# Decoder layer on one core: routing's norm and turns of 12 of 16 token tiles moved into the cross-attention stage

## The chip, the cores and the metric

One core of a Trainium2 chip. The metric is the device time of one execution in microseconds; lower is better. TensorE (PE), VectorE (DVE), ScalarE (ACT), GpSimd (POOL) and SyncE (SP) run their own instruction lists and meet in semaphores; 16 DMA engines move the data.

## The reference

```python
x = x + attention(_layernorm(x), ...)        # 16 heads, ternary weights, int8-like activations
x = x + cross_attention(_layernorm(x), ctx_1024, Wq, Wk, Wv, Wo, gq, gk)   # 16 heads of 128
xf = _layernorm(x).reshape(-1, 256)
logits = xf @ router_w.T                     # 8 experts
top_v, top_i = jax.lax.top_k(logits, 2)
combine = sum(one_hot(top_i, 8) * softmax(top_v)[..., None], axis=1)
y = einsum('etf,ehf->eth', silu(xf @ gate_w[e].T) * (xf @ up_w[e].T), down_w)
x = x + einsum('te,eth->th', combine, y)
```

x is 32 x 64 x 256 in float32: 2048 tokens, 16 tiles (`NT`) of 128 tokens by 256 channels. F is 688. Float32 accuracy is kept by writing a number as a sum of two float16 halves and taking three of the four products.

## The kernel before

Three stages follow each other, each an `nc.Block` in which every engine has its own list, and a barrier between them.

`attention` (to about 209 us) is not touched.

`cross_attention` works on 4 groups (`NG`) of 4 tiles. Two heads of a group make a pair, 8 pairs (`NU`) a group, 32 pairs in all. A loop over steps N from -9 to 32 is written out for each engine by hand, and the order of the calls in it is the order on the engine. In step N the pair N+9 is projected (queries, keys), pair N+1 gets its scores and softmax, and pair N is multiplied with the context and projected out (`project_out`). For N from 24 (`TAIL`) no projections are left: these are the tail's steps, in which the turned probabilities come from TensorE and ScalarE (`turn_p`, `turned_copy`) and not from a DMA. After the last pair of a group VectorE adds the result to x (`residual`, steps 8, 16, 24, 32), and SyncE saves the group's rows of x to the output (`save_group`).

Beside it the weights of the experts are split in 67 pieces of 128x512: SyncE loads a piece, ScalarE makes the high half (`piece_high`), VectorE or GpSimd the low half (`piece_low`; odd ones, and the first 16 both, on GpSimd), SyncE saves both halves to `w_hl` and then issues the load of a later piece (`piece_save`, L795). Two pieces belong to each step from -8 (`piece_at`, L709), so the last, 66, falls into step 25. On ScalarE `piece_high` stands at the head of a step (L1045 to L1050). On SyncE the norms of the keys go out and come back broadcast (`key_norms_out`, `key_norms_in`) behind the step's saves; GpSimd's `both_norms` waits for them, and its `quotient` stands behind that. In step 26 SyncE loads the down weights of four experts (`first_down_weights`).

`experts` begins with routing. VectorE takes the moments of all 16 tiles (`token_stats`), ScalarE the root, VectorE writes the normed rows to `ao` (L1649). TensorE turns them in pairs of tiles in float32 (L1778), ScalarE copies the turned tiles out, TensorE multiplies with the router's weights (L1786); between these stand products whose result nobody reads (`idle_work`, L1765). ScalarE and VectorE split the rows in halves (L1595, L1653), and two DMAs save them to `h_rows` (L1599). A chain on VectorE picks the top two and gives each token a place in one of 39 slots of 128 rows. SyncE has issued the gate and up weights at the stage's start (L1520); ScalarE issues the down weights of the other four experts once the top two are known (L1603 to L1607). Then for every slot: GpSimd gathers the rows (L1557), SyncE turns them (L1525), TensorE multiplies with gate and up (L1825) and down (L1841), and GpSimd adds the result to the output (L1572).

## Time and profile before

| | us |
|---|---|
| median of 3 runs | 852.17 (851.31 to 855.72) |
| profiled execution | 852.5 |
| its span | 850.4 |
| step -1 of cross-attention | 260.61 to 274.44 |
| tail, from the first turn to the last product | 517.99 to 569.3 |
| routing, from the moments to the first expert product | 570.89 to 622.79 |

Times in the rows count from the span's start. Busy shares over the span are PE 85%, DVE 67%, ACT 53%, POOL 45%; they mix stages with different limits.

### The profile page before, as it was taken

The numbers are of one execution on the slowest core, as the hardware profiler recorded it, in microseconds if no ns is written. First come the engines' busy times: TensorE is split into PE (matmuls) and PEld (weight loads), VectorE is DVE, ScalarE is ACT, GpSimd is POOL, SyncE is SP. The second block draws the span as 40 slices with busy tenths as digits, with TensorE's granted clock in tenths as the row PEclk, the third lists the DMA queues.
The fourth block names the chain that finished last, engine by engine and source line by source line (L and its number), as shares of the span: only waits on it lengthen the run. The fifth ranks groups of instructions, "written<-read, shape, count | busy, mean of one in ns | idle before, by whom it ended". The sixth has DMA issues, their size and how long they took to land. (4 is left out here: it accounts for less than half of the span.)

```text
span 850.4 us, 26921 instructions
## 1 busy us (share of the span) xinstructions
PE 722.7 (85%) x10796; PEld 522.1 (61%) x10796; DVE 568.7 (67%) x1052; ACT 453.9 (53%) x875; POOL 382.5 (45%) x462
## 2 busy tenths in 40 slices
PE   0499888887887999999999996988199999998993
PEld 0388777775443566656556664766167777776772
DVE  5778788863886989999898997967853333332330
ACT  0567777764785666667675763544023333333331
POOL 0112222322585555555555555620056666665753
PEclk9879999995998999999999998999599999999997
DMA  9312222321664757576757573619949988889882
GB/s 323 112 50 56 59 52 64 66 58 20 168 194 156 186 127 180 135 187 160 191 128 173 163 167 112 223 31 406 369 89 158 149 147 143 142 128 137 145 140 40
DMA packets 192471, 121.91 MB, mean 143 GB/s; under 512 B 140800, under 2 KB 172800, under 8 KB 192224
## 3 DMA queue, kind: packets, MB, share of 16 engines
q1 hardware_dynamic: 178928, 103.54, 50.3%
q0 software_dynamic: 7488, 9.32, 7.1%
q10 hardware_dynamic: 5936, 7.34, 2.5%
q8 instruction: 90, 1.47, 0.7%
q14 instruction: 29, 0.24, 0.1%
HBM read 61.04 MB, written 27.00 MB: 104 GB/s over the span
## 5 line engine op out<-in xcount | busy, mean ns | idle before, releaser
L1754 DVE SCALAR_TENSOR_TENSOR f_slot_work<-psu,f_slot_work 128x688 f32<-128x688 f32 x39 | 34.1, 875 | 109.8 <-PE psu L1825 109.8
L1350 PE MATMUL xbank_a<-arena,x_o 128*128 128x256 f16 x768 | 96.6, 277 | 5.7 <-DVE x_o L1155 2.9
L1572 POOL DMA_INDIRECT out_dram<-f_y,f_to x39 | 62.2, 1595 | 71.8 <-DMA out_dram<-f_y,f_to 55.4
L1350 PEld LDWEIGHTS xbank_a<-arena,x_o 128*128 128x128 f16 x768 | 73.4, 99 | 28.7 <-DVE x_o L1155 10.3
L1254 PE MATMUL xbank_qk<-arena 128*128 128x512 f16 x336 | 84.8, 390 | 4.6 <-PEq L188 4.3
L1841 PE MATMUL fbank<-arena,f_slot_work 128*128 x663 | 79.2, 274 | 3.3 <-DMA f_slot_work<-hid_hl 3.3
L1825 PE MATMUL psg<-wgu,f_slot_work 128*128 x468 | 74.7, 309 | 2.5 <-DMA f_slot_work<-rows_in 2.0
L1825 PE MATMUL psu<-wgu,f_slot_work 128*128 x468 | 74.6, 309 | 0.0
L1841 PEld LDWEIGHTS fbank<-arena,f_slot_work 128*128 128x128 f16 x663 | 64.7, 98 | 14.6 <-issue 4.3
L1622 ACT CAST hid_hl<-f_slot_work 128x688 f16<-128x688 f32 x39 | 29.8, 765 | 77.4 <-DVE f_slot_work L1754 75.4
L915 POOL TENSOR_TENSOR arena<-arena,cst 128x512 f32<-128x512 f32 x25 | 26.0, 1039 | 92.2 <-DVE cT L1190 92.2
L961 ACT ACTIVATE sqq<-xbank_qk 128x512 f32<-128x512 f32 x56 | 33.3, 595 | 56.3 <-PE xbank_qk L1254 56.3
L1615 ACT ACTIVATE f_slot_work<-psg 128x688 f32<-128x688 f32 x39 | 29.0, 743 | 64.4 <-PE psg L1825 63.1
L545 PE MATMUL bank_pt<-cst,sp 64*64 64x64 f32 x1024 | 42.8, 242 | 21.6 <-ACT pT L321 19.4
L1825 PEld LDWEIGHTS psg<-wgu,f_slot_work 128*128 128x128 f16 x468 | 45.4, 98 | 23.4 <-issue 3.8
L1825 PEld LDWEIGHTS psu<-wgu,f_slot_work 128*128 128x128 f16 x468 | 45.8, 98 | 22.5
L1757 DVE TENSOR_TENSOR hid_hl<-f_slot_work,hid_hl 128x688 f16<-128x688 f32 x39 | 34.2, 877 | 32.4 <-ACT hid_hl L1622 32.4
L545 PEld LDWEIGHTS bank_pt<-cst,sp 64*64 64x64 f32 x1024 | 38.4, 154 | 23.9 <-issue 20.5
L1254 PEld LDWEIGHTS xbank_qk<-arena 128*128 128x128 f16 x336 | 28.7, 99 | 36.8 <-issue 8.0
L1145 DVE TENSOR_TENSOR q_hl<-xbank_qk,q_hl 128x512 f16<-128x512 f32 x56 | 38.4, 686 | 16.9 <-ACT q_hl L962 16.9
L1262 PE MATMUL xbank_qk<-cT,wk 128*128 128x512 f16 x168 | 47.1, 391 | 0.0
L904 POOL TENSOR_TENSOR x_pf<-x_sc,x_rden 128x512 f32<-128x512 f32 x32 | 33.4, 1042 | 29.8 <-DVE x_rden L1178 29.8
(285 smaller groups left out, 1717.5 us busy)
## 6 DMA issues: line engine op xcount, KB each, us to landing
arena<-in_wx SPq DMA_DIRECT2D x51, 256.0 KB, 3.0
wgu<-w_hl SPq DMA_DIRECT2D x2, 5504.0 KB, 26.5
ao<-key_norms SPq DMA_DIRECT2D x64, 128.0 KB, 3.3
w_hl<-cT SPq DMA_DIRECT2D x26, 256.0 KB, 2.1
w_hl<-x_pair SPq DMA_DIRECT2D x25, 256.0 KB, 2.2
ao<-in_wx SPq DMA_DIRECT2D x10, 256.0 KB, 3.2
w_hl<-ao SPq DMA_DIRECT2D x10, 256.0 KB, 2.1
x_sb<-in_x SPq DMA_DIRECT2D x4, 512.0 KB, 9.6
```

Of the source, the lines that this page charges most:

```text
L545: last = nc.tensor.matmul(pt[rows, n * S:(n + 1) * S], sp[i % 2][rows, 8 * part + n, :], cst[rows, IDENT + S * b:IDENT + S * b + S], start ...
L904: nc.gpsimd.tensor_tensor(pf[:, :, :], sc[n % 2][:, :, :], rden[n % 2][:, :].unsqueeze(2).to_broadcast([P, 2 * GT, S]), ALU.mult).then_inc ...
L961: nc.scalar.activation(sqq[h % 2][:, :], query_bank(h), ACT.Square, scale=1.0 / (H_UP * W_UP)).then_inc(sq_done, 1)
L1145: nc.vector.tensor_tensor(q_hl[:, 1, slot(h), :], query_bank(h), q_hl[:, 0, slot(h), :], ALU.subtract).then_inc(lq_done, 1)
L1254: last = nc.tensor.matmul(query_bank(h), wq[:, a, k, f:f + D2], hT[:, g, b * NCH + k, :], start=(j == 0), stop=(j == len(terms) - 1))
L1262: last = nc.tensor.matmul(key_bank(h), wk[:, a, f:f + D2], cT[:, g, b, :], start=(j == 0), stop=(j == 2))
L1350: last = nc.tensor.matmul(acc[t // 2][:, (t % 2) * C:(t % 2 + 1) * C], o_hl[h % 2][:, a, at:at + P], wvo[:, b, e, :], start=(e == 0 and j ...
L1572: nc.gpsimd.indirect_dma_start(out=dram["out_rows"], out_offset=bass.IndirectOffsetOnAxis(ap=to[n % 2][:, 0:1], axis=0), in_=y[n % 2][:, : ...
L1754: nc.vector.scalar_tensor_tensor(out=h3, in0=psu[:, :].rearrange("p (c n) -> p c n", c=2)[:, :, 0:FH], scalar=HID_UP / (H_UP * W_UP), in1= ...
L1757: nc.vector.tensor_tensor(hid_hl[n % 2][:, 1, 0:FF], hid[n % 2][:, :], hid_hl[n % 2][:, 0, 0:FF], ALU.subtract).then_inc(s["hh_low"], 1)
L1825: last = nc.tensor.matmul(bank[:, c * 512:c * 512 + FH], xT[n % 2][:, b * NCH + k, :], wgu[:, bass.ds(e, 1), at:at + FH].rearrange("p a n ...
L1841: last = nc.tensor.matmul(ps[n % 2][:, 0:C], hidT[n % 3][:, a, f, :], wd[:, bass.ds(e, 1), at:at + C].rearrange("p a n -> p (a n)"), start ...
```

## The change

The norm, the halves, the save to `h_rows` and the turn of tiles 0 to 11 (`ROUTED`) move into `cross_attention`, as pairs j = 0 to 5 of tiles. `routed_moments` on VectorE in steps 9, 11, 17, 19, 25, 26; `routed_h` and `routed_high` on ScalarE in steps 13, 14, 21, 22, 27, 28; `routed_low` on GpSimd one step later; `save_rows` on SyncE two steps later, one save and two turns. The turned halves lie where x lay, after `save_group` has saved it. The router's weights are loaded and split there too. In `experts` only the last 4 tiles are normed and turned; the 12 others go straight into products of float16 halves with 8 columns. `idle_work` ahead of and between the turns is gone (the one before the slots stays). The down weights are issued on SyncE right behind gate and up. The low halves of the last rows stand behind the top two.

Step -1 (`REST_AT`) has no pieces, and all later ones are one step later, so the last falls into step 26. For N from 24 the pieces stand last in a step on ScalarE, GpSimd and (behind the sums) VectorE. `save_group(2)` moves from step 27, where it stood behind the down weights, to step 25.

```diff
-        first_step = 1 - AHEAD
+        first_step, REST_AT = 1 - AHEAD, -1
         def piece_at(N, r):
-            return 2 * (N - first_step) + r
+            if N == REST_AT:
+                return -1
+            return 2 * (N - first_step - (N > REST_AT)) + r
+        def routed_stats(N):
+            g, r = divmod(N - 1, NU)
+            if g == NG - 1:
+                return [j for j in (RPAIRS - 2 + r,) if r < 2]
+            return [2 * (g - 1) + r // 2] if 1 <= g and r in (0, 2) else []
+        def routed_rows(N):
+            g, r = divmod(N - 1, NU)
+            if g == NG - 1:
+                return RPAIRS - 4 + r if 2 <= r < 4 else None
+            return 2 * (g - 1) + r - 4 if 1 <= g and r in (4, 5) else None
+        def routed_save(N):
+            return routed_rows(N - 2)
...
+                def save_rows(j):
+                    sp.wait_ge(r_low_done, j + 1)
+                    sp.dma_start(h_rows[.. tiles 2j, 2j+1], hp_of(j)).then_inc(r_saved[j % 2], 16)
+                    for a in range(2):
+                        sp.dma_start(x_sb[:, 2 * j + a, :] as F16, hp_of(j)[:, a], transpose=True).then_inc(r_saved[j % 2], 16)
...
-                    if N > 2 and (N - 3) % NU == 0 and 0 < N // NU < NG:
+                    if N > 2 and N < TAIL and (N - 3) % NU == 0 and 0 < N // NU:
                         save_group(N // NU - 1)
                     if N == TAIL + 2:
                         first_down_weights()
+                    if routed_save(N) is not None:
+                        save_rows(routed_save(N))
                     for r in range(2):
                         if piece(piece_at(N, r)):
                             piece_save(piece_at(N, r))
+                    if N == TAIL + 1:
+                        save_group(NG - 2)
...
+                def routed_h(j):
+                    part = slice(2 * j, 2 * j + 2)
+                    act.wait_ge(r_stats_done, 2 * j + 2)
+                    routed.step(nc.scalar.mul(r_minus[:, part], r_mv[:, part, 0], -1.0))
+                    routed.link(nc.scalar.activation(r_ln[:, part], r_mv[:, part, 1], ACT.Ln, bias=...))
+                    nc.scalar.activation(r_rstd[:, part], r_ln[:, part], ACT.Exp, scale=-0.5, bias=...).then_inc(r_norm_done, 1)
+                    act.wait_ge(r_norm_done, j + 1)
+                    for t in (2 * j, 2 * j + 1):
+                        nc.scalar.mul(r_minus[:, t:t + 1], r_minus[:, t:t + 1], r_rstd[:, t:t + 1]).then_inc(r_shift_done, 1)
+                    act.wait_ge(group_saved, (j // 2 + 1) * 16)
+                    act.wait_ge(r_shift_done, 2 * j + 2)
+                    for a in range(2):
+                        t = 2 * j + a
+                        nc.scalar.activation(rows_of(j)[:, a, :], x_sb[:, t, :], ACT.Identity, scale=r_rstd[:, t:t + 1], bias=r_minus[:, t:t + 1]).then_inc(r_rows_done, 1)
+                def routed_high(j):
+                    act.wait_ge(r_rows_done, 2 * j + 2)
+                    if j >= 2:
+                        act.wait_ge(r_saved[j % 2], j // 2 * 48)
+                    nc.scalar.copy(hp_of(j)[:, :, 0, :], rows_of(j)).then_inc(r_high_done, 1)
...
                 # ScalarE, steps from TAIL
                         if pair(n + 1):
                             exponent(n + 1)
+                        if routed_rows(N) is not None:
+                            routed_h(routed_rows(N))
+                            routed_high(routed_rows(N))
+                        for r in range(2):
+                            if piece(piece_at(N, r)):
+                                piece_high(piece_at(N, r))
...
                 # VectorE, steps from TAIL
                         if pair(n + 1):
                             shifted(n + 1)
-                        if piece(piece_at(N, 0)):
-                            piece_low(piece_at(N, 0))
                         if pair(N):
                             out_low(2 * N)
                         if pair(n + 1):
                             sums(n + 1)
+                        if piece(piece_at(N, 0)):
+                            piece_low(piece_at(N, 0))
+                        for j in routed_stats(N):
+                            routed_moments(j)
...
                 # SyncE, experts
                 for l in range(2):
                     sp.dma_start(wgu[...], weights[l, :, :, 0:GUC]).then_inc(s["gate_up_in"], 16)
+                for part in (slice(0, 1), slice(1 + EARLY_DOWN, NE)):
+                    sp.dma_start(wd[:, part, ...], ...).then_inc(s["down_in"], 16)     # the four DMAs that ScalarE issued
...
                 # TensorE, experts
-                idle_work(ps[3], 32)
...
+                for t in range(ROUTED):
+                    turned = x_sb[:, t, :].bitcast(F16).rearrange("p (l k n) -> p l k n", l=2, k=NCH)
+                    for j, (k, a, b) in enumerate(terms):
+                        nc.tensor.matmul(ps[2][:, t * NE:(t + 1) * NE], turned[:, a, k, :], wr_hl[:, b, k, :], ...)
```

## Rows read from the trace of the kernel before

**Rows 1.** The page's head.
```profile
span 850.4 us, 26921 instructions
```
**Rows 2.** Busy time by stretch; the row of columns first.
```profile
core 0: us, PE busy (x) PEld busy (x) DVE busy (x) ACT busy (x) POOL busy (x), PEclk, DMA share, GB/s
260.61:274.44 13.83, 9.32 (x103) 3.79 (x100) 7.59 (x13) 6.49 (x14) 6.45 (x7) 0.75 0.50 154
284.35:294.47 10.12, 9.83 (x175) 6.27 (x172) 9.12 (x15) 6.51 (x13) 5.47 (x6) 1.00 0.84 188
355.24:366.34 11.10, 9.93 (x174) 6.17 (x170) 10.14 (x17) 6.62 (x13) 5.54 (x6) 1.00 0.57 152
540.56:545.93 5.37, 5.24 (x128) 4.28 (x129) 5.13 (x9) 3.13 (x5) 3.65 (x4) 1.00 0.91 300
610.00:614.50 4.50, 2.50 (x31) 1.99 (x32) 4.43 (x7) 0.46 (x1) 0.00 (x0) 0.50 1.03 401
```
**Rows 3.** Instructions in order of time, step -1: start, us, engine, line, idle before.
```profile
260.38 0.54 SPq L793 DMA_DIRECT2D ao<-in_wx  x1
...
263.81 0.63 ACT L1010 ACTIVATE ao<-ao 128x512 f16<-128x512 f32 x1 [3.83 <-DMA ao<-in_wx]
...
266.51 0.48 PE L1281 MATMUL xbank_n<-cst,x_logs 128*128 128x128 f32 x1 [3.55 <-ACT x_logs L976]
...
268.54 2.74 PE L1254 MATMUL xbank_qk<-arena 128*128 128x512 f16 x6 [0.27 <-DVE q_hl L1145]
```
**Rows 4.** The same view, steady steps 1 and 2, and step 8's residual.
```profile
289.40 1.47 PE L1254 MATMUL xbank_qk<-arena 128*128 128x512 f16 x6
...
296.85 0.60 ACT L961 ACTIVATE sqq<-xbank_qk 128x512 f32<-128x512 f32 x1 [1.73 <-PE xbank_qk L1254]
...
361.96 1.28 DVE L1184 SCALAR_TENSOR_TENSOR x_sb<-xbank_a,x_sb 128x512 f32<-128x512 f32 x2
```
**Rows 5.** Durations of like operations, by line (busy us, mean ns; ns min/median/max).
```profile
L297 ACT ACTIVATE u<-u,cst,qsc 128x256 f32<-128x256 f32 x48 | 25.3, 592 | 12.0 <-DVE deq L432 12.0
...
L1030 ACT ACTIVATE per_pair<-k_hl,cst x3: 279/296/296, 211.1 to 237.1; 128x2 f32<-128x2 f32 x3
...
L1121 DVE BATCH_NORM_STATS2 stats_o<-x_sb 128x6 f32<-128x256 f32 x6 | 2.2, 415 | 3.2 <-PEq L188 3.2
```
**Rows 6.** Instructions in order of time, tail.
```profile
528.39 2.37 SPq L819 DMA_DIRECT2D ao<-key_norms  x4
...
530.07 0.63 ACT L1010 ACTIVATE cT<-arena 128x512 f16<-128x512 f32 x1 [4.52 <-DMA arena<-in_wx]
...
537.57 1.04 POOL L904 TENSOR_TENSOR x_pf<-x_sc,x_rden 128x512 f32<-128x512 f32 x1 [2.26 <-DVE x_rden L1178]
...
544.82 1.61 DVE L1169 TENSOR_TENSOR x_sc<-x_sc,x_mx 128x512 f32<-128x512 f32 x1
...
546.46 0.63 ACT L996 ACTIVATE x_sc<-x_sc 128x512 f32<-128x512 f32 x1 [1.32 <-DVE x_sc L1169]
...
548.16 0.68 DVE L1155 SCALAR_TENSOR_TENSOR x_o<-xbank_qk,x_o 128x512 f16<-128x512 f32 x1
```
**Rows 7.** The chain that ended last, routing: start, us, what.
```profile
570.89 5.34 DVE f_stats L59 x16
...
580.29 0.44 PE fbank L1778 x4
...
593.16 0.30 DVE logits L1656
...
616.98 3.06 DMA rows_in<-h_rows,f_at
620.05 2.50 DMA f_slot_work<-rows_in
...
622.79 1.92 PE psg L1825 x12
...
626.47 1.73 PE fbank L1805 x32
```
**Rows 8.** DMAs from issue to landing: all saves of rows; a group's save (min/median/max).
```profile
h_rows<-f_slot_work ACTq DMA_DIRECT2D x2, 1024.0 KB, 15.9
...
DMA to landing us min/median/max: 3.9/5.2/11.2
```

More of the change, by code:

```diff
@@ L53, in link @@
         self.settle()
-def token_stats(nc, chain, v, stats, mv):
-    for t in range(NT):
-        chain.step(nc.vector.bn_stats(stats[:, t, :], v[:, t, :]))
-    chain.settle()
-    for t in range(NT):
-        chain.step(nc.vector.bn_aggr(mv[:, t, :], stats[:, t, :]))
-    chain.settle()
 W_UP = 64.0
@@ L931, in _ @@
                         piece_low(piece_at(N, 0))
-                    if piece(piece_at(N, 1)):
+                    if N < TAIL and piece(piece_at(N, 1)):
                         piece_low(piece_at(N, 1))
@@ L953, in _ @@
                         quotient_low(n + 1)
+                    if N >= TAIL and piece(piece_at(N, 1)):
+                        piece_low(piece_at(N, 1))
+                    if routed_rows(N - 1) is not None:
+                        routed_low(routed_rows(N - 1))
             @block.scalar
@@ L1044, in _ @@
                     n, m = N + 1, N + AHEAD
-                    if piece(piece_at(N, 0)):
+                    if N < TAIL and piece(piece_at(N, 0)):
                         piece_high(piece_at(N, 0))
@@ L1048, in _ @@
                         out_high(2 * N - 1)
-                    if piece(piece_at(N, 1)):
+                    if N < TAIL and piece(piece_at(N, 1)):
                         piece_high(piece_at(N, 1))
@@ L1190, in piece_low, with routed_moments @@
                     nc.vector.scalar_tensor_tensor(out=halves(i)[:, 1, :], in0=raw(i), scalar=W_UP, in1=halves(i)[:, 0, :], op0=ALU.mult, op1=ALU.subtract).then_inc(low_even, 1)
+                routed = Chain(dve, r_step_dve)
+                def routed_moments(j):
+                    dve.wait_ge(x_done, j // 2 * 2 + j % 2 + 1)
+                    for a in range(2):
+                        routed.step(nc.vector.bn_stats(r_stats[:, a, :], x_sb[:, 2 * j + a, :]))
+                    routed.settle()
+                    for a in range(2):
+                        nc.vector.bn_aggr(r_mv[:, 2 * j + a, :], r_stats[:, a, :]).then_inc(r_stats_done, 1)
                 for N in steps:
@@ L1597, in _ @@
[L1597 to L1607 removed]
+                links = Chain(act, s["act_step"])
@@ new lines, in _ @@
+                for u in range(GT // 2):
+                    pair = slice(2 * u, 2 * u + 2)
+                    act.wait_ge(s["stats_ready"], 2 * u + 2)
+                    links.link(nc.scalar.activation(root[:, pair], mv[:, pair, 1], ACT.Ln, bias=cst[:, CONSTS:CONSTS + 1]))
+                    nc.scalar.activation(rstd[:, pair], root[:, pair], ACT.Exp, scale=-0.5, bias=cst[:, CONSTS + 6:CONSTS + 7]).then_inc(s["roots_ready"], 1)
+                for u in range(GT // 2):
+                    act.wait_ge(s["t_done"], u + 1)
+                    nc.scalar.copy(hTf[u][:, 0].rearrange("p a k n -> p (a k n)"), ps[u][:, :]).then_inc(s["t_copied"], 1)
@@ new lines, in _ @@
+                for u in range(GT // 2):
+                    nc.scalar.copy(hp[:, 2 * u:2 * u + 2, 0:C], ao[:, ROUTED + 2 * u:ROUTED + 2 * u + 2, :]).then_inc(s["hh_ready"], 1)
+                act.wait_ge(s["hl_ready"], GT // 2)
+                act.dma_start(dram["h_rows"].rearrange("(t p) c -> p t c", p=P)[:, ROUTED:, :], hp[:, :, :]).then_inc(s["h_saved"], 16)
+                act.wait_ge(s["mask_ready"], 2)
+                nc.scalar.activation(top[1][:, :], top[1][:, :], ACT.Exp, scale=1.0 / (H_UP * W_UP)).then_inc(s["exp_done"], 1)
@@ new lines, in _ @@
+                for u in range(GT // 2):
+                    pe.wait_ge(s["t_copied"], u + 1)
+                    pe.wait_ge(s["t_lows"], u + 1)
+                    for a in range(2):
+                        t = ROUTED + 2 * u + a
+                        for j, (k, l, b) in enumerate(terms):
+                            last = nc.tensor.matmul(ps[2][:, t * NE:(t + 1) * NE], hTf[u][:, l, a, k, :], wr_hl[:, b, k, :], start=(j == 0), stop=(j == len(terms) - 1))
+                    last.then_inc(s["l_done"], 1)
```

154 lines of the change are left out of this document (93 added, 61 removed).

## The prediction

> **What bounds the kernel now.** First the page's head [rows 1] gives the span of 850.4 us. That run took 852.5 us, so 2.1 us lie outside the span, and it stood 0.3 us above the median of 852.17 us. I sum changes of the span and apply them to the median.
>
> Then the stretches of equal kind [rows 2]. Cross-attention takes 260.61 to 570.9 in steps. A steady step is 10.12 us with PE 9.83 busy and DVE 9.12: TensorE sets the pace, VectorE is just below. A step with a residual update takes 11.10 with PE nearly unchanged at 9.93: its 1.28 us on VectorE [rows 4] show almost whole. A tail step is 5.37 us with PE 5.24 and DVE 5.13: both full. Step -1 is 13.83 us with only 9.32 of PE: something stops it. Then routing: 570.89, when the moments begin, to 622.79, the first expert product [rows 7], 51.9 us in which no expert works. Behind it come 39 expert slots, which the change does not touch; whatever moves 622.79 moves the end.
>
> **Step -1, which loses its two pieces.** The loads of pieces 14 and 15 are issued late, the second at 260.38. ScalarE's `piece_high`, at the head of the step, waits 3.83 us for the first until 263.81, then 1.03 more for the second. The logs stand behind it, and TensorE stops for 3.55 us. After that its six query products take 2.74 us [rows 3] and not 1.47 [rows 4]: the granted clock averages 0.75 in this step [rows 2], part of it at the lower level, 1.2 GHz. With the pieces in step 0, ScalarE takes the query product when PE ends it, near 263.0 and not 266.7. Gain 3.7 plus 1.3 for the slow products plus 0.2 of others: 5.2 us; bounds 3.5 (the wait alone) and 6.5 (the squares' products at full clock too). By then the loads have landed. GpSimd does both halves of pieces 14 and 15 in step 0, 4.4 us, which fits before the quotient of that step. The key norms for heads 8 to 15 come after these two saves, at the time of before, since they did so behind piece 17.
>
> The Trainium skill (TensorE: Matmul & The Clock Gate, part 1) has the same direction: a busy array is given the full clock and an idle one falls back. By it alone the slow products would be gained too; the rows already say so.
>
> **Steps 9 to 22, which gain work.** Per pair of tiles VectorE gets two bn_stats of 415 ns and two aggregates: 1.0 us, in steps 9, 11, 17, 19. ScalarE gets three tiny operations, a Ln and an Exp near 0.30 each, two Identity of 128x256 at 592 ns, and a cast of 0.6 [rows 5]: with hand-offs 2.8 us at the end of steps 13, 14, 21, 22. GpSimd gets one subtract of 1.16 us (idle there). SyncE gets one save and two turns, about 2.9 us of issuing, ahead of the piece saves of steps 15, 16, 23, 24; the saves start 0.6 us later, while the piece loads have about 1 us to spare.
> Before each query copy ScalarE waits 1.73 us for TensorE [rows 4]: it absorbs most of 2.8 us and hands on about 1. VectorE has half a us idle at the end of a step and hands on 0.5. Part of both dies in the turn's waits. Bounds: 0, if all is absorbed, and 4 x (1.0 + 2.8) = 15.2, if all shows, as the residual's 1.28 did. I take 3.0, about 0.4 for each of 8 places, since the wait of 1.73 us lies right behind the added work and the residual has none behind it.
>
> **The tail, steps 24 to 32.** Three things move against each other.
> - Before, ScalarE stood 4.52 us for the load of piece 66 at the head of step 25 [rows 6]. Now the pieces stand behind the exponent. But one step without pieces means five pieces in the tail, not three. GpSimd's `piece_low(63)` now stands behind `quotient_low(26)`, so SyncE saves piece 63 near 532 and not 528, and the key norms of heads 56 to 63 leave behind it, 533 and not 528.39 [rows 6]. GpSimd's product of step 25 needs them (3.3 to 4 us to land, so near 537), and the quotient is queued behind it: it started at 537.57 before [rows 6] and would start near 538.1 now. So the stall of 4.52 us isn't won: another of the same length arrives. Net about +0.6 at step 27.
> - VectorE gets one more piece (0.69) and two pairs of moments (2.0) in steps 24 to 26, about 1.7 of it in step 26, where it is full (its subtract alone is 1.61 us beside GpSimd [rows 6]).
> - ScalarE gets its 2.8 us in steps 27 and 28, right after the exponent. The next out_high stands behind it, and VectorE waits for that. Before, exponent at 546.46, out_low at 548.16 [rows 6], between them 0.54 to reach out_high and 0.6 for it: slack 0.6. So 2.2 us each, 4.4.
> Sum 6.7. Some of it should be absorbed by the better order in steps 24 to 26, so I take 5.0. Bounds: -4 (the stall of 4.52 is won and all else hides) and +9 (the group's save, which ScalarE now also awaits, lands late: such saves took 3.9 to 11.2 us to land [rows 8]).
>
> **Routing.** From T0 = 570.89 to the logits at 593.16 are 22.3 us [rows 7]. New chain: 72 small products of the 12 turned tiles at 54 ns (32 in 1.73 [rows 7]) are 3.9; statistics and rows of the four last tiles lie beside them. Then eight transposes 2 x 0.44, the second copy 0.6, its low half 0.7, 12 products 0.65, hand-offs 0.9: T0 + 7.6. Minus 14.7. The low halves of the rows, two at 0.69, now stand between mask and sums; the 1.2 us of TensorE's sums cover all but 0.2. So by the chain alone -14.5, and the gather that started at 616.98 starts at 602.5.
> But the DMA engines are full until 614.4: busy share 1.03 up to there [rows 2]. Removed are 1.5 MB of row saves (two of 1 MB [rows 8], now one of 0.5), at the 401 GB/s of that stretch 3.7 us. They drain at 610.7. The turn of the first rows is issued on SyncE's queue, where the down weights now lie before it. Before, a group's save behind down weights landed after 11.2 us, the median being 5.2 [rows 8]: a queue serves in order. So the turn runs from 610.7, 2.50 us, and the first product is at 613.4: -9.3. The turn waits, not the chain of VectorE. TensorE, its filler done near 607.7, is then idle over 5 us, more than the 3.55 of step -1, and its first products run slow: I put 1.3 of a possible 2.2 us (twice 1.47 to 2.74 less 0.3). Route -8.0; bounds -14.5 and -7.
> The Trainium skill (DMA: Bandwidth & Descriptors, Queues, rings and completion order) says that descriptors are consumed in ring order within a queue, while queues interleave. By it the turn waits as I assume, and the save of the last rows, on ScalarE's queue, does not; the save of 11.2 us agrees.
> That filler work is gone (32 + 16 products) matters little: at the lower clock the 96 small products and transposes cost some 4 us more, which the drain of the DMA covers.
>
> **Sum.** -5.2 + 3.0 + 5.0 - 8.0 = -5.2 us. 852.17 - 5.2 = 847.0 us; its own range 843 to 851.
>
> **Rivals.**
> 1. *The tail gives nothing back.* Pieces last in a step free ScalarE, and its 2.8 us lie in waits. For it: ScalarE is busy 3.13 of 5.37 us in a tail step [rows 2]. Against it: what stands behind the added work is due within 0.6 us. Tail 0: 842.
> 2. *The turn is not held by the down weights*, because engines drain unevenly or the loads end early. Route -14: 841. Against it the 11.2 us.
> 3. *The other side: the steady steps have no slack.* The place is steps 9 to 22, the price 15.2 instead of 3.0, and the precedent is the residual [rows 2, 4]. -5.2 + 15.2 + 5.0 - 8.0 = +7.0: 859. It decides from the point where the added work costs over 8.2 us there, half of its length. Against it: 1.73 us of waiting before each query copy.
> 4. *Step -1 keeps its time*, because another wait of the same length (the first score's chain, the norms) is there once the piece is gone: 852.2.
>
> **How the numbers follow.** Main case 0.45 (0.28 faster by over 0.5%, 0.17 within); rival 1 0.22; rival 2 0.07; rival 3 0.09; rival 4 0.12 (0.11 within, 0.01 slower); 0.05 for the rest (0.03 slower, 0.02 within). That is 0.57 faster, 0.30 within, 0.13 slower. 0.5%, 4.3 us, is about what a measurement of this kernel tells from none. The range 840.5 to 853.5 takes in rivals 1, 2 and 4, and leaves out rival 3 and the worst of the tail.
>
> **What would show it.** Step -1: about 8.6 us long, no ScalarE wait for a load, granted clock near 1. Steps 9 to 22: together up to 3 us longer than before. Tail: ScalarE or GpSimd still waiting near step 25 for a load or key norms; steps 27 and 28 about 2 us longer each, VectorE waiting for out_high. Routing: logits 8 us after the block's start, gather near 32 us, the first row turn landing only when the down weights have, first product near 42.5 to 44 us, slow at first. I am wrong if the tail from its first turn is as short as before, if the turn lands within 3 us of the gather while weights still flow, or if any steady step grows by the full length of what it gained.

## The result, and the profile after: slower, where 5 us less were forecast

The changed kernel takes 861.25 us (median of 20 runs, 852.90 to 864.15), the kernel before in the same comparison 851.87 (846.40 to 855.72): ratio 1.0095, 95% interval 1.0073 to 1.0116. Forecast were 847.0 us and a range to 853.5. A later comparison of the same two kernels (g2_after_again, below) gave 1.0045 (1.0013 to 1.0077). The two intervals together say a loss of 0.1 to 1.2%. The kernel before, timed against itself in that later comparison, came out at 1.0039, so the size of the loss is uncertain by some 0.4%. Neither set shows a gain.

The profiled run of after took 861.95 us. Its head, then the busy time by stretch (columns as in [rows 2]): step -1, steady step 3, step 8 with its residual, steps 14 and 15, and routing's second half.

```profile
span 860.0 us, 26893 instructions
```
```profile
core 0: us, PE busy (x) PEld busy (x) DVE busy (x) ACT busy (x) POOL busy (x), PEclk, DMA share, GB/s
266.85:275.15 8.30, 6.48 (x103) 3.25 (x100) 7.58 (x13) 5.13 (x11) 1.48 (x2) 1.00 0.44 139
306.20:317.07 10.87, 9.94 (x175) 6.41 (x172) 9.12 (x15) 7.37 (x16) 5.47 (x6) 1.00 0.61 125
357.08:368.19 11.11, 9.94 (x175) 6.18 (x172) 10.14 (x17) 6.63 (x13) 5.54 (x6) 1.00 0.57 157
418.39:430.79 12.40, 10.18 (x174) 6.10 (x171) 8.85 (x15) 9.28 (x21) 5.33 (x6) 1.00 0.52 144
430.79:443.00 12.21, 10.33 (x176) 6.24 (x172) 8.84 (x15) 9.91 (x20) 6.50 (x7) 1.00 0.71 154
```
```profile
617.00:624.00 7.00, 4.22 (x18) 1.89 (x19) 6.35 (x21) 0.00 (x0) 3.92 (x6) 0.53 1.02 402
624.00:631.00 7.00, 1.38 (x7) 0.41 (x5) 1.97 (x3) 0.00 (x0) 1.29 (x1) 0.95 1.16 355
```

Step -1 is 8.30 us and no longer 13.83, at the full clock throughout. Step 8 is as long as in [rows 2]. Steps 14 and 15 are the news: 12.40 and 12.21 us with no more than 0.4 us more of TensorE's work in them, VectorE less busy than in a steady step, ScalarE some 3 us busier. In routing the compute engines run out of work while the DMA engines are full: their share is 1.02 to 1.16 until 631.

To see what is chance I cut every profile at the same places: a step begins at its first score product, routing at its first bn_stats, the slots at the first expert product. The table holds all eighteen, in us (the first column is the start of step -1, all of it attention and early steps that no kernel here changes; "rest" is the span from there on; the ratio is to the kernel before, timed in the same comparison).

| kernel | reaches -1 | step -1 | 0-8 | 9-22 | 23 and tail | routing | slots | rest | ratio |
|---|---|---|---|---|---|---|---|---|---|
| before | 260.6 | 13.8 | 91.9 | 142.3 | 62.2 | 51.9 | 227.6 | 589.8 | 1 |
| g3_before_again | 262.6 | 15.7 | 93.2 | 142.3 | 61.7 | 51.8 | 225.8 | 590.4 | 1.0039 |
| b4_before_shifted | 262.5 | 15.4 | 92.3 | 141.3 | 63.0 | 51.7 | 226.2 | 590.0 | 1.0017 |
| g1_down_on_sync | 259.8 | 13.8 | 92.4 | 142.2 | 63.4 | 52.1 | 225.3 | 589.3 | 1.0008 |
| d1_rest_alone | 265.3 | 8.3 | 93.7 | 140.5 | 64.5 | 51.8 | 229.4 | 588.1 | 0.9974 |
| after | 266.9 | 8.3 | 93.0 | 150.1 | 71.6 | 43.1 | 227.0 | 593.1 | 1.0095 |
| g2_after_again | 262.8 | 8.3 | 92.8 | 149.5 | 71.5 | 43.1 | 226.9 | 592.1 | 1.0045 |
| g4_down_on_scalar | 260.8 | 8.3 | 93.3 | 150.5 | 73.1 | 43.1 | 227.6 | 595.9 | 1.0074 |
| e3_down_later | 267.6 | 8.3 | 92.9 | 149.3 | 71.1 | 36.4 | 234.3 | 592.3 | 1.0086 |
| e4_rest_undone | 259.0 | 14.9 | 92.4 | 150.1 | 71.3 | 43.1 | 227.5 | 599.3 | 1.0119 |
| e2_block_short | 263.9 | 8.3 | 94.0 | 147.5 | 69.3 | 43.1 | 227.3 | 589.5 | 1.0025 |
| e1_block_moved | 261.5 | 8.3 | 93.4 | 147.1 | 69.6 | 43.0 | 227.6 | 589.0 | 1.0032 |
| b2_tail_short | 263.1 | 8.3 | 93.5 | 146.9 | 67.7 | 43.0 | 226.3 | 585.6 | 0.9997 |
| b3_tail_order | 258.1 | 8.3 | 93.4 | 147.0 | 72.5 | 42.9 | 226.1 | 590.2 | 1.0051 |
| b1_down_split | 263.9 | 8.3 | 92.9 | 146.6 | 70.2 | 38.4 | 229.2 | 585.6 | 0.9980 |
| c3_b1_norms_first | 258.0 | 8.3 | 92.8 | 146.6 | 69.8 | 38.4 | 232.6 | 588.6 | 1.0008 |
| c1_holes | 262.5 | 8.3 | 93.9 | 143.6 | 67.9 | 38.4 | 229.6 | 581.9 | 0.9925 |
| c2_norms_first | 263.1 | 8.3 | 93.7 | 143.5 | 65.8 | 38.4 | 230.7 | 580.4 | 0.9902 |

The first column is a warning. Before and after differ in it by 6.2 us, as much as by the stages that the change touches, and it is chance of one execution: thirteen profiles of after and its variants reach step -1 at 258.0 to 267.6 (mean 262.4), five of before and its variants at 259.8 to 265.3 (mean 262.2). Steps 9 to 22, by contrast, repeat within 1.8 us between kernels whose work is equal there, "23 and tail" within 1.7 us (before, g3, b4, g1), and steps 0 to 8 within 1.3 us. From step -1 on, before and its repeat take 589.8 and 590.4, after and its repeat 593.1 and 592.1: 2.5 us more.

### What stands in steps 14 and 15

The instructions of after in order of time, end of step 14 and start of step 15 (start, us, engine, line, in brackets the idle time before and what ended it). L1100 to L1116 are `routed_h` and `routed_high`, L1029 is `out_high`, L1249 `out_low`.

```profile
429.38 0.20 ACT L1100 ACTIVATE per_pair<-per_pair 128x2 f32<-128x2 f32 x1
...
430.70 1.09 ACT L1110 ACTIVATE x_sb<-x_sb,per_pair 128x256 f32<-128x256 f32 x2
...
431.82 0.62 ACT L1116 CAST arena<-x_sb 128x512 f16<-128x512 f32 x1
432.35 0.62 ACT L1067 ACTIVATE cT<-arena 128x512 f16<-128x512 f32 x1
432.88 0.58 ACT L1029 ACTIVATE x_o<-xbank_o 128x512 f16<-128x512 f32 x1
...
433.48 0.69 DVE L1249 SCALAR_TENSOR_TENSOR x_o<-xbank_o,x_o 128x512 f16<-128x512 f32 x1 [3.15 <-ACT x_o L1029]
...
434.39 0.33 PE L1392 MATMUL xbank_n<-cst,x_logs 128*128 128x128 f32 x1 [1.25 <-ACT x_logs L1033]
```

Read from the bottom: TensorE waits for the logs, which stand behind the block too; VectorE has stood still for 3.15 us, since its first instruction of a step is `out_low(2N-1)` and its queue is in order; `out_high` stands behind a piece and the block, 2.97 us long. A step earlier the same `out_low` waits 2.95, and a query product then waits 1.31 us for the low half of the query, which VectorE has done late (first fence). Step 14 was long already in the kernel before, 11.37 us, because TensorE waits there for a turn of the probabilities (second fence, before); the change adds only 1.0 us to it, and 2.3 to step 15, 2.5 to step 22 and 2.1 to step 23, which took 9.9 to 10.1.

```profile
421.27 0.69 DVE L1249 SCALAR_TENSOR_TENSOR x_o<-xbank_o,x_o 128x512 f16<-128x512 f32 x1 [2.95 <-ACT x_o L1029]
...
425.27 1.04 PE L1365 MATMUL xbank_qk<-arena 128*128 128x512 f16 x4 [1.31 <-DVE q_hl L1239]
```
```profile
422.03 0.52 PE L1337 MATMUL xbank_o<-x_pT,ck 64*128 64x64 f16 x24 [1.54 <-DMA x_pT<-x_p]
```

The tail of after. The key norms that left at 528.39 in [rows 6] leave at 545.85, 15 us into step 24 where it was 10, and GpSimd waits 6.59 us for them; ScalarE waits 4.14 us for a late piece, beside GpSimd's wait and not behind it (the two end at 549.48 and 551.44); from step 27 on `out_low` waits for the block again.

```profile
545.85 2.37 SPq L852 DMA_DIRECT2D ao<-key_norms  x4
549.48 0.63 ACT L1067 ACTIVATE x_pair<-arena 128x512 f16<-128x512 f32 x1 [4.14 <-DMA arena<-in_wx]
...
551.44 1.06 POOL L946 TENSOR_TENSOR ao<-ao,rec_q 128x512 f32<-128x512 f32 x1 [6.59 <-DMA ao<-key_norms]
...
565.77 0.69 DVE L1249 SCALAR_TENSOR_TENSOR x_o<-xbank_qk,x_o 128x512 f16<-128x512 f32 x1 [2.32 <-ACT x_o L1029]
```

Routing of after, from the chain that ended last (start, us, what). It answers to [rows 7]: logits 6.6 us after the start at 589.96 and not 22.3, gather 30.4 and not 46.1.

```profile
596.51 0.30 DVE logits L1772
...
620.32 6.26 DMA rows_in<-h_rows,f_at
626.59 6.23 DMA f_slot_work<-rows_in
633.05 3.62 PE psg L1943 x12
```

Gather and turn, 3.06 and 2.50 us in [rows 7], are 6.26 and 6.23 beside the weights, and the first twelve products, which come after 7.67 us of idling on TensorE, take 3.62 us and not 1.92: the granted clock is 0.50 from 633 to 636.7.

### The profile page after: what moved, and what is told of

The parts are those of the page before. It is cut to its first block and busy times, and to the rows that moved or that the text cites. A ratio compares the mean times of both kernels' runs of the same rounds, so it can differ in the third digit from the quotient of the medians.

```text
span 860.0 us, 26893 instructions
## 1 busy us (share of the span) xinstructions
PE 714.9 (83%) x10756; PEld 517.3 (60%) x10756; DVE 558.4 (65%) x1035; ACT 461.9 (54%) x914; POOL 389.5 (45%) x468
## 5 line engine op out<-in xcount | busy, mean ns | idle before, releaser
L1461 PE MATMUL xbank_a<-arena,x_o 128*128 128x256 f16 x768 | 99.7, 282 | 7.7 <-DVE x_o L1249 5.0
L1943 PEld LDWEIGHTS psg<-wgu,f_slot_work 128*128 128x128 f16 x468 | 46.1, 99 | 29.4 <-issue 8.9
L1249 DVE SCALAR_TENSOR_TENSOR x_o<-xbank_o,x_o 128x512 f16<-128x512 f32 x55 | 37.7, 685 | 23.2 <-ACT x_o L1029 23.2
L231 POOL TENSOR_SCALAR kd<-cst,deq 128x128 f32<-128x128 f32 x16 | 10.4, 649 | 86.2 <-PE bank_g L576 55.9
L1239 DVE TENSOR_TENSOR q_hl<-xbank_qk,q_hl 128x512 f16<-128x512 f32 x56 | 38.4, 686 | 13.7 <-ACT q_hl L1019 13.4
## 6 DMA issues: line engine op xcount, KB each, us to landing
wgu<-w_hl SPq DMA_DIRECT2D x2, 5504.0 KB, 25.4
```

Of the source, the lines that this page charges most:

```text
L1239: nc.vector.tensor_tensor(q_hl[:, 1, slot(h), :], query_bank(h), q_hl[:, 0, slot(h), :], ALU.subtract).then_inc(lq_done, 1)
L1249: nc.vector.scalar_tensor_tensor(out=o_hl[h % 2][:, 1, :].rearrange("p (b n) -> p b n", b=2), in0=ob_of(h)[:, :, 0:RW], scalar=1.0 / P_UP, ...
L1461: last = nc.tensor.matmul(acc[t // 2][:, (t % 2) * C:(t % 2 + 1) * C], o_hl[h % 2][:, a, at:at + P], wvo[:, b, e, :], start=(e == 0 and j ...
L1943: last = nc.tensor.matmul(bank[:, c * 512:c * 512 + FH], xT[n % 2][:, b * NCH + k, :], wgu[:, bass.ds(e, 1), at:at + FH].rearrange("p a n ...
```

## The experiments

### Is it the block's place? e1_block_moved, e2_block_short

e1 takes the block from the end of a step and puts it into the next, behind `out_high`; e2 leaves it in its place and does its three long operations on 8 of 256 columns, leaving the other columns out.

```
 e1   (end of step N)                        (step N, behind out_high and the second piece)
-  if routed_rows(N) is not None:         +  if N < TAIL and routed_rows(N - 1) is not None:
-      routed_h(routed_rows(N))           +      routed_h(routed_rows(N - 1))
-      routed_high(routed_rows(N))        +      routed_high(routed_rows(N - 1))
 e2
+  few = slice(0, C if j > 3 else 8)      # both Identity and the cast
```

> The kernel after, with ScalarE's routed block (routed_h and routed_high, 3.0 us) of steps 13, 14, 21 and 22 taken from the end of its step and put into the next one, behind out_high and the second piece and ahead of the query's square. Theory: what costs in these steps is that out_high(2N-1) stands behind the block and VectorE's first instruction, out_low(2N-1), waits for it (2.95 to 3.16 us in the kernel after). Steps 13 to 15 and 21 to 23 took 61.2 us before and 70.2 after; moved, they fall to 62 to 65, and the whole by 5 to 8 us. The 1.73 us wait ahead of the query copy takes most of the block; what is over shows. Rival: the steps grow because SyncE's save and turns and the added DMA traffic delay pieces and turned quotients: then they stay at 69 to 71 and the time stays. Attention up to step -1 is free to tell whether its 6.2 us of difference are chance: 260.6 before, 266.9 after.

> The kernel after, with the two Identity operations and the cast of ScalarE's block in steps 13, 14, 21 and 22 done on 8 columns of 256 (the first eight tiles' rows are left out but for these columns); SyncE's saves and turns and VectorE's moments stay. The block falls from about 3.0 to 1.6 us. Theory: steps 13 to 15 and 21 to 23 fall from 70.2 us to about 64 (each of the four places keeps half of its cost), the whole by 5 to 6. Rival (SyncE's queue and the DMA): they stay at 69 to 71.

Measured: steps 13 to 15 and 21 to 23 took 64.5 us in e1 and 66.5 in e2 (70.2 in after and 69.1 to 70.0 in the four other profiles with after's order, 61.2 before). Timed, e1 is at 1.0032 (1.0005 to 1.0059), e2 at 1.0025 (0.9996 to 1.0055); against after that is 1 to 5 us less by its two timings, for 5 to 8 expected. The same 3.0 us of work, moved behind three instructions in each of four places, cost some 5 us less in all (4.6 to 5.7). SyncE's saves and turns and the DMA traffic are the same in all three kernels, so the rival falls. e2 kept a little more than expected: the five tiny operations are most of what is left of it (0.2 to 0.3 us each).

What e1 still pays is told by the same rule. In step 14 its block costs nothing (11.29 us, 11.37 before). In step 15 the logs stand between the block and the query, TensorE waits for them, and the step takes 11.77 us, 9.91 before:

```profile
428.99 0.33 PE L1392 MATMUL xbank_n<-cst,x_logs 128*128 128x128 f32 x1 [1.68 <-ACT x_logs L1033]
```

### Does it hide in parts? c1_holes

```
+ parts = {(12, 0): "n0", (12, 1): "a0", (13, 0): "b0 h0", (14, 0): "n1", (14, 1): "a1", (15, 0): "b1", (15, 1): "h1",
+          ...
+          (26, 0): "n4", (27, 0): "n5", (28, 0): "a4 b4", (29, 0): "h4 a5", (30, 0): "b5 h5"}
  # n: norm, a and b: the two rows, h: cast, with the pair's number;
  # place 0: ahead of query(2m) (tail: behind out_high(2N)), place 1: ahead of query(2m+1)
+ lows = {14: 0, 15: 1, 22: 2, 23: 3, 29: 4, 30: 5}   # GpSimd's low half; SyncE saves a step later
```

> b1_down_split with ScalarE's routed block no longer in one piece: its norm, its two rows and its cast stand in the places where ScalarE waits anyway (ahead of the two query products' squares in steps 12 to 15 and 20 to 23; between out_high(2N) and the exponent in steps 26 to 30). Theory: what costs is the length of the block ahead of an instruction that another engine awaits, so the parts of at most 1.25 us hide in waits of 0.8 to 1.7 us. The tail from the end of step 22 to the start of routing (71.6 us in the kernel after, 70.2 in b1_down_split, 62.2 before) falls by 3 to 5, steps 13 to 15 and 21 to 22 by another 1 to 2. Whole: 4 to 6 us under b1_down_split. Rival: ScalarE has no room in the tail, any place costs its 3 us: the tail stays at 69 to 71.

Measured: 0.9925 (0.9896 to 0.9954), 846.08 us. Steps 9 to 22 are 143.6 us, 1.3 above before; steps 13 to 15 take 31.1, as before (31.2). What is left is where VectorE's moments fall: a third of a us in steps 12 and 20, some 0.8 in step 18. In step 15 of c1 the parts stand in waits, and VectorE's `out_low` at the head of step 16, behind them, waits 0.27 us (L1114 is a row, L1120 the cast, L1020 the query's square, L1031 `out_high`, L1264 `out_low`):

```profile
427.40 0.58 ACT L1114 ACTIVATE x_sb<-x_sb,per_pair 128x256 f32<-128x256 f32 x1
428.52 0.60 ACT L1020 ACTIVATE sqq<-xbank_qk 128x512 f32<-128x512 f32 x1 [0.53 <-PE xbank_qk L1380]
...
431.55 0.61 ACT L1120 CAST arena<-x_sb 128x512 f16<-128x512 f32 x1
432.45 0.60 ACT L1020 ACTIVATE sqq<-xbank_qk 128x512 f32<-128x512 f32 x1 [0.29 <-PE xbank_qk L1380]
...
436.21 0.69 DVE L1264 SCALAR_TENSOR_TENSOR x_o<-xbank_o,x_o 128x512 f16<-128x512 f32 x1 [0.27 <-ACT x_o L1031]
```

Step 23 and the tail fell by 2.3 us only, for 3 to 5 expected. The next experiments say why.

### What the tail pays for: b2_tail_short, b3_tail_order, e4_rest_undone, d1_rest_alone

The first two stand on e1, e4 on after, d1 on before.

```
 b2 + few = slice(0, C if j < 4 else 8)                            # in steps 27, 28
 b3   piece_high, piece_low of the tail at the head of a step again, on all three engines
 e4 - first_step, REST_AT = 1 - AHEAD, -1
    + first_step, REST_AT = 1 - AHEAD, NPAIR + 1                   # after: two pieces in step -1 again
 d1 + if N == REST_AT:                                             # before: this part alone
    +     return -1
    + return 2 * (N - first_step - (N > REST_AT)) + r
```

> e1_block_moved with the two Identity operations and the cast of ScalarE's block in steps 27 and 28 done on 8 columns of 256 (rows of tiles 8 to 11 are left out but for these). Start of step 24 to the start of routing: 52.2 us before, 59.4 in e1_block_moved. Theory: ScalarE's block costs 4.4 of these 7.2 us; it shrinks from 3.0 to 1.6 us, so the tail falls to about 57. Rival: late loads and key norms of the added tail pieces and the order of the pieces cost it all: it stays at 59.

> e1_block_moved with the tail pieces of ScalarE, VectorE and GpSimd back where the kernel before has them, at the head of a step and ahead of the quotient. Theory: pieces last in a step let GpSimd save late, so key norms come late, but free ScalarE's head; the two cancel, and the tail stays within 1.5 us of 59.4. Rival: the new order itself is what costs, the tail falls to 55 to 57. Second rival: the new order is what saves (five pieces at the head would stall ScalarE and TensorE by 4 to 8 us more): 62 to 67.

> The kernel after, with two pieces in step -1 again (REST_AT moved out of range), so three tail pieces instead of five; they still stand last in a tail step. Theory: step -1 grows from 8.3 back to 13.8 us with ScalarE's wait of 3.8 us for a load; the tail (start of step 24 to routing, 52.2 before, 59.4 after) falls by 2 to 4 us, since the wait of 4.14 us for the load of piece 65 and the late key norms belong to the added pieces. Whole: +1.5 to +4 us. Rival: the tail's loss is all from ScalarE's block in steps 27 and 28 and the moments: the tail stays at 59 and the whole is +5.5.

> The kernel before with one part of the change alone: step -1 without pieces (so five pieces in the tail, in the order of before). Theory: step -1 falls from 13.8 to 8.3 us; steps 9 to 22 stay; the tail (62.2 us from the end of step 22) grows by 2 to 5 us, since the key norms leave behind two more saves. Whole: -1 to -4 us. Rival: the two pieces cost nothing in the tail, whole -5.5. Beside it: x's last quarter is there by 13.3 us as in the two profiles of the kernel before's line, or at 17.3 to 18.5 as in all of the kernel after's line; in the first case attention takes what it took before.

Measured, step 23 and tail together (e1, the base of the first two, has 69.6):

- b2 has 67.7, 2.0 us less where ScalarE has 2.8 us less work. Counted from step 24 as in the expectation it is 57.4 where e1 has 59.4, on the forecast.
- b3 has 72.5, 2.8 more: putting the pieces last saves, which I had thought a draw.
- d1 has 64.5 where before has 62.2 and the other kernels with before's tail 61.7 to 63.4: five pieces in place of three cost 1 to 3 us. Step -1 gives 5.5 (13.83 to 8.29) or more, since the other profiles with pieces in it have 13.8 to 15.7. Its time is 0.9974 (0.9941 to 1.0007).
- e4's step -1 is 14.9 us again, but its tail 71.3, only 0.3 under after. So the rival was nearer there. Taking the two pieces out again gives nothing while the block is whole; that the pieces' delay then lies beside the block's is my reading of it, and no run singles it out.

### The next wait in the tail: c2_norms_first, c3_b1_norms_first

```
+ for part in range(2):                     # ahead of save_rows and of the pieces' saves
+     if N >= TAIL and batch(N - 1 - part) is not None:
+         key_norms_in(batch(N - 1 - part), part)
```

> c1_holes with SyncE's loads of the last key norms ahead of its saves of rows and pieces in steps 24 and 25. Theory: they then leave when the score of step 23 has read the tile, 10 us earlier than 538 in b1_down_split; GpSimd's wait of 5.4 us for them in step 25 goes, and 2 to 5 us of it reach the end (ScalarE's wait of 3.5 us for a piece's load is next). Rival: the load of the piece holds ScalarE for as long, less than 1 us is won. Second rival: the saves and loads of pieces, now later, hold ScalarE longer and it is slower.

> b1_down_split with SyncE's loads of the last key norms ahead of its saves in steps 24 and 25, ScalarE's block left where it is. It tells the effect of the key norms from that of the block: theory, the tail falls by 2 to 5 us from 70.2; rival, by less than 1.

Measured: with the block in its parts the tail falls by 2.1 us (67.9 to 65.8), and c2 is at 0.9902 (0.9869 to 0.9934), 844.89 us; with the block whole (c3) by 0.4, which is the rival's figure. From b1's 70.2 us, then, the norms alone give 0.4, the block in parts alone 2.3 (c1), and both together 4.4: most of what the earlier norms are worth shows only when the block is out of their way. In c1 (first fence) the norms leave at 533.59 and GpSimd waits 6.42 us; in c2 (second) they leave at 519.93, GpSimd waits for them no more, and ScalarE's wait for a piece is left.

```profile
533.59 4.15 SPq L854 DMA_DIRECT2D ao<-key_norms  x4
...
539.01 1.06 POOL L948 TENSOR_TENSOR ao<-ao,rec_q 128x512 f32<-128x512 f32 x1 [6.42 <-DMA ao<-key_norms]
```
```profile
519.93 2.97 SPq L854 DMA_DIRECT2D ao<-key_norms  x4
...
537.37 0.63 ACT L1072 ACTIVATE x_pair<-arena 128x512 f16<-128x512 f32 x1 [3.40 <-DMA arena<-in_wx]
```

### Routing: e3_down_later, b1_down_split, g4_down_on_scalar, g1_down_on_sync

```
 e3  (on after)  down weights issued on SyncE behind turn_rows(1)
 b1  (on e1)     + down_weights(slice(0, 1))                       # where after has them
                 + if n == -1:                                     # behind turn_rows(1)
                 +     down_weights(slice(1 + EARLY_DOWN, NE))
 g4  (on after)  down weights on ScalarE's queue behind the mask, as before
 g1  (on before) down weights on SyncE's queue behind gate and up, this part alone
```

> The kernel after, with SyncE's eight loads of down weights issued behind the turns of the first two slots' rows instead of ahead of them. Theory: in the kernel after the gather (6.3 us) and the row turn (6.2 us) share the DMA engines and the queue with the down weights. With them behind, gather and turn take 3.1 and 2.5 us as before, the first product comes 36.5 to 38 us after the block's start instead of 43.2, and the slots may wait 0 to 3 us for the first down weights. Whole: -3 to -8 us. Rival: gate and up weights (11 MB) themselves fill the DMA until about 28 us after the start and the gather is bound by something else: the first product stays at 42 to 43. Second rival: SyncE's issue of eight loads delays the first hidden turn and gives back all that is won.

> e1_block_moved with the down weights of expert 0 issued where the kernel after has them and those of experts 5 to 7 behind the turns of the first two slots. Theory: in e3_down_later gather and turn were quick (first product 36.4 us after the block's start), and the 7 us came back because the third slot's row turn was issued at 633.0, behind eight loads, and landed last (TensorE idle 7.13 us). With four loads fewer there, the first product comes at 36.5 to 38 us after the start, the third slot waits 0 to 3 us, and routing and slots together fall from 270.6 to 263 to 267; the whole is 3 to 7 us under e1_block_moved. Rival: the row turns of slots 2 and 3 wait for the down weights on the DMA engines whatever the issue order: routing and slots stay at 270.

> The kernel after with the down weights back on ScalarE's queue behind the mask. Theory: gather (issued about 30 us after the start) still runs beside the weights and takes 5 to 7 us, the turn of the rows too if weights are still on their way; issued later, they land later, so the first product comes 42 to 45 us after the start and routing and slots together stay within 2 us of 270.0. Rival: only the order within SyncE's queue holds the turn; then the turn takes 2.5 us and the first product comes at 38 to 40. Beside it: x's last quarter at 17.3 us or later as in all of this line, unless the queue of the down weights is its cause, then by 13.4.

> The kernel before with one part of the change alone: the down weights issued on SyncE behind gate and up, not on ScalarE behind the mask. Theory: the DMA engines are full from the block's start to 43 us behind it in any case; down weights in the same queue come no later, and in before the gather starts only 46 us after the start, when all has landed. So routing takes 47 to 52 us (51.9 before) and the whole is within 0.5% of before. Rival: the row turn stays held by weights in its own queue and routing grows. Beside it, of x's last quarter: if the load that moved to SyncE's queue is what delays x in the kernel after's line (17.3 to 18.5 us, against 13.3), x is late here too; otherwise it is there by 13.4.

Measured: g1 leaves routing at 52.1 us and the time at 1.0008 (0.9976 to 1.0040): nothing by itself. In g4 the weights are on another queue and the first product is still 43.1 us behind the start, with turn and gather as long as in after, by the chain of waits:

```profile
616.40 6.14 DMA rows_in<-h_rows,f_at
622.56 6.31 DMA f_slot_work<-rows_in
629.11 3.62 PE psg L1943 x12
```

The packets show where the time goes. In before the gather's first packet moves 1.9 us after its issue and the turn's 1.2; in after and in g4 these are 4.4 to 4.5 and 3.1 us. So 2.6 of the gather's 3.2 added us, and 1.9 of the turn's 3.7, pass before anything of it moves. In g4, from 622.6 to 625.4, one packet of SyncE's queue went out and 467 of ScalarE's queue with the weights.

e3 brings the first product at 36.4 us, and pays it all back: its third row turn lies behind eight loads, and TensorE stands 7.13 us for it (first fence, e3); routing and slots are 270.7 us for after's 270.1. b1 leaves 1.18 us of that wait (second fence) and has 267.6, just above the 263 to 267 expected.

```profile
641.65 3.62 PE L1946 MATMUL psg<-wgu,f_slot_work 128*128 x12 [7.13 <-DMA f_slot_work<-rows_in]
```
```profile
632.06 1.92 PE L1946 MATMUL psg<-wgu,f_slot_work 128*128 x12 [1.18 <-DMA f_slot_work<-rows_in]
```

b1's 3.0 us are not safe: the four kernels with that order have slots of 229.2 to 232.6, the others but e3 of 225.3 to 229.4, so on average (269.0 for 270.1) 1 us is left.

### What is chance: g2_after_again, g3_before_again, b4_before_shifted

```
 b4 + unused = sb("unused", [P, 2, NCH, NE], F16)    # before, at wr_hl's place
```

> The kernel after, unchanged. What attention took in its first profile, 266.9 us to the start of step -1 against 260.6, is to be told from chance: eleven profiles of its line reached step -1 at 258.0 to 267.6 us, mean 262.5. Theory: this one lies near 262.5, 4 us under the first, with the steps from step -1 on taking the same as in the first profile within 1.5 us; the time is 0.7 to 1.2% over before. Rival: 266 to 267 again, then the kernel after's attention is slower by itself.

> The kernel before, unchanged: a second profile of it for the same question. Theory: step -1 starts between 258 and 266 us, x's last quarter is there by 13.4 us, the time is within 0.3% of itself.

> The kernel before with an unused tile of 64 bytes a partition allocated where the kernel after allocates wr_hl, so every tile behind it lies 64 bytes further on. In five profiles of the kernel after and its variants x's last quarter landed at 17.4 to 18.5 us, in the one of before by 13.3, with the DMA engines busy and moving 116 to 215 GB/s for a while; the five reached step -1 at 259.0 to 267.6 us, before at 260.6. Theory: the shift of addresses does that: x's last quarter lands after 17 us here too, and the whole is 2 to 5 us slower than before. Rival: it is chance of a run, or belongs to the program's length: x is there by 13.3 us, and the time is that of before within 0.2%.

Measured: g2 reaches step -1 at 262.8 and repeats every stage from there within 1 us, as expected, though its ratio, 1.0045, is under the 0.7% expected. g3 is the kernel before itself and came out at 1.0039 (1.0006 to 1.0073), where I had expected it within 0.3%: two sets of runs of one program can differ by 0.4% here, and the intervals are a little too narrow. b4 gave 1.0017 (0.9979 to 1.0056) and x in time: the shifted addresses are not it.

One thing is no chance of one run. VectorE's last bn_stats on x, in before (first fence) and after (second):

```profile
13.34 4.01 DVE L396 BATCH_NORM_STATS2 stats<-x_sb 128x6 f32<-128x256 f32 x12
```
```profile
18.02 1.41 DVE L386 BATCH_NORM_STATS2 stats<-x_sb 128x6 f32<-128x256 f32 x4 [2.11 <-DMA x_sb<-in_x]
```

All thirteen profiles of after's line wait for x in these statistics (1.4 to 2.9 us), and of before's five one, g1, by 0.26. It costs 1 to 2.5 us at that place. The part of it that reaches the end isn't to be seen in the first column, whose spread is larger. The timed ratios of after's line lie 0.2 to 5 us above what the table's "rest" gives, 2.5 on average, but those of before's own variants lie -0.5 to 2.7 above it too, 1.2 on average. Its cause is open: neither the addresses (b4), nor step -1 (d1), nor the queue of the down weights (g4 still waits) is it.

## Why the prediction was wrong

**Step -1.** The account was right: -5.2 us forecast, -5.5 measured in the profiled runs, no wait for a load, clock at 1. Steps 0 and 1 gave back 1.1 us (9.91 and 10.12 became 10.36 and 10.78) that I had not counted; g3, with before's steps, took 10.72 and 9.95, so part of it may be chance.

**Steps 9 to 22: the step that failed.** Forecast +3.0, measured +7.8, and another 2.1 in step 23 by the same block, which stands at the end of step 22. Together 9.9 us, beyond the 8.2 from which rival 3 decides; its 859 was the nearest to the result, though its precedent, a residual on VectorE, was not the reason. VectorE's moments were priced about right (some 1.4 us in all, where 0.4 or 0.5 a place was forecast). ScalarE's block was not: I wrote that the wait of 1.73 us ahead of the query copy takes most of 2.8 us, "since the wait lies right behind the added work". It does not. Between them stands `out_high(2N-1)`, and in steps 15 and 23 the logs, each awaited by an engine that is nearly full. The 1.73 us were there in the trace and are real: e1's step 14, where the same block stands directly ahead of that wait, and c1, in parts, get them. The slack that counts is that of the first instruction behind the added work for which another engine waits. I had read no line of `out_high`; measured, its slack was nil, for a block of 2.97 us made `out_low` wait 2.95 to 3.16. In the tail I had used that very rule and found 0.6 us; I did not apply it to the steady steps.

**The tail from step 24.** +5.0 forecast, +7.3 measured, inside the bounds of -4 and +9. The parts stood nearly as told. From turn to turn steps 24 to 26 took 25.9 us for 22.6 before, 3.3 more where 0.6 and 1.7 were forecast: a stall for key norms in place of the one for a load, and more. Steps 27 to 30 took 25.4 for 21.5, 3.8 more where 4.4 were forecast for the block. Nothing of the 6.7 was absorbed on the whole, and two sizes in the first part were off. The key norms left 27 us after the start of step 23, not 24, and SyncE's save and turns of the fourth pair stand ahead of the pieces' saves there (c2, with the norms ahead of them all, has them leave 14 us earlier than c1). And a load was late after all (4.14 us), at the same time as the key norms. "Some of it should be absorbed by the better order" was right in kind (2.8 us by b3).

**Routing.** -8.0 forecast, -8.8 measured, the first product at 43.1 us for 42.5 to 44 forecast, slow at first. The figure held, its reason only in half. I let the turn lie behind the down weights in their queue until 610.7 and then take 2.5; measured are a gather and a turn both slowed, by 3.2 and 3.7 us, on whichever queue the weights are (g4). The weights in flight decide, and not their place in one queue. I had leaned on what the Trainium skill (DMA: Bandwidth & Descriptors, Queues, rings and completion order) says of queue order. By g4 that order is not needed for the delay.

The same section of the Trainium skill says that a transfer's semaphore increment lands only after every earlier write of that DMA engine, across its queues. That could account only for what comes behind a transfer's last packet: in g4 the turn's last packet moves 5.0 us after the issue and the landing follows 1.3 us later, in before at 1.95 and 0.55. What keeps the first packet back in g4 stays open.

**The sum.** By the profiled runs from step -1 on: -5.5 +1.1 +7.8 +2.1 +7.3 -8.8, and -0.7 in the slots: +3.3 where -5.2 were forecast. That is 0.4%, and would by itself lie outside the range (855.5 for 853.5). The timed +0.95% and +0.45% lie above it, by 5 us and by some 1. The late x may be part of the difference, and two sets of runs of one program differ by 0.4%; where the rest of the first set's 5 us went the profiles don't show.

**Rivals.** Rival 1 (the tail gives nothing back) and 4 (step -1 keeps its time) are out. Rival 2's condition, that the turn isn't held by the weights, is met only when they are issued later, and then they hold a later turn. I gave rival 3 a chance of 0.09; the residual, whose 1.28 us show almost whole in a full step, should have raised it.

## The version that beats both

c2_norms_first keeps what the change does and moves four things: ScalarE's block into the waits, the tail's rows one to two steps later, the key norms ahead of the saves, part of the down weights behind two turns. It takes 0.9902 (0.9869 to 0.9934) of the kernel before's time, in one set of runs; the gain of 1.0% is over twice the 0.4% by which two sets of one program differed. By stages it has the whole of step -1 (-5.5) and routing (-13.5, of which the slots take back 3), pays 1.8 us in steps 0 to 8, 1.2 in 9 to 22, and 3.6 in step 23 and the tail, of which some 2.3 are the added pieces by d1.

## What to carry to other kernels

Work added to an engine in order has the slack of the first instruction behind it that a busy engine awaits, not that of the next long wait on its own row; go down the queue instruction by instruction to the first dependent. If the work has no deadline, cut it up and put each part directly ahead of a wait. When two delays lie side by side, undoing one can show almost nothing (c3: 0.4 us) and still be worth more once the other is gone (c2 on c1: 2.1), so undo them together before calling one harmless. And before a stage's difference is explained, look at how far it spreads over profiles of kernels that are equal there.

## What the hardware showed

- A 3 us gather and a 2.5 us turn became 6.1 to 6.3 us each beside 400 GB/s of other loads, whether these were on the turn's own queue or on another. Of the added time, 2.6 and 1.9 us passed before the first packet moved.
- In attention's first microseconds the DMA engines can move less while a load is due: x's last quarter was issued by 3.7 us in after and awaited until 18.0. The fences show 10 to 12.4 us: after (first: busy share in tenths of 40 slices, then packets and mean rate) and before (second). From 11.4 us on the share falls to 1 to 3 tenths in five of seven slices of 0.06 us; I had called the engines busy in an expectation, by a coarser view. It is no chance of one run: from 10 to 14 us the thirteen profiles of after's line move 241 to 278 GB/s, the five of before's line 300 to 344. What the engines wait for the trace does not tell.

```profile
DMA  9999999899989999998999991217392859969789
...
DMA packets 647, 0.61 MB, mean 254 GB/s; under 512 B 51, under 2 KB 647, under 8 KB 647
```
```profile
DMA packets 839, 0.80 MB, mean 332 GB/s; under 512 B 62, under 2 KB 839, under 8 KB 839
```
